# A graph network in four layers: the edge term of a pair added in one operation, sums of two pairs joined, weights stored behind the values

## The chip, the cores and the metric

The kernel runs on one core of a Trainium2 chip. The metric is the time on the device in microseconds; before the change it is 4184.97 us (median of 3 runs, 4182.91 to 4187.28).

## The reference

Four layers follow one another on 3125 nodes of 256 features and 53125 edges, sorted by destination. Each is `x = layernorm(x + layer(x))`. The change touches the fourth alone, two transformer convolutions with a ReLU between them, with 4 heads of 64 channels:

```python
def _transformer_conv(x, src, dst, edge_attr, Wq, bq, Wk, bk, Wv, bv, We, be, Ws, bs):
    q = (x @ Wq + bq).reshape(n, H, C)
    k = (x @ Wk + bk).reshape(n, H, C)
    v = (x @ Wv + bv).reshape(n, H, C)
    e = (edge_attr @ We + be).reshape(-1, H, C)
    k_j = k[src] + e
    q_i = q[dst]
    alpha = jnp.einsum('ehc,ehc->eh', q_i, k_j) / jnp.sqrt(C)
    ...
    msg = (v[src] + e) * alpha[..., None]
    out = jax.ops.segment_sum(msg, dst, num_segments=n)
    return out.reshape(n, H * C) + x @ Ws + bs
```

The dots stand for the softmax of `alpha` over the edges of one destination. The same edge term `e` is added to the key and to the value of an edge.

## The kernel before, in words

The program is a list of phases. The last five are `finish2` (end of the third layer, with the first projection), `attend(1)`, `between` (end of the first convolution, second projection), `attend(2)` and `last_rows`. A projection (`Projection`) makes queries, keys, values and skip terms; keys and values go to the table `kv_tab` in HBM, one row of 516 floats for a node: 256 of the key, then four heads of 64 value channels and one zero each (`KVW`, L42).

`attend` works on 440 tiles of 128 edges, two tiles making a pair, 220 pairs. A pair goes through these stations:

- The edge term, `aT` times `we`, is a product on TensorE into one of two PSUM banks (`edge_terms`, L1950).
- The gather of the 128 rows `kv_tab[src]` of a tile is an indirect DMA that GpSimd issues, one for a tile. There are two kinds. For an odd pair (`plain(p)`) it is plain (L1775): the rows land in the slots of `kv`, and VectorE adds the edge term afterwards, once to the keys (L1801) and once to the values (L1803). For an even pair ScalarE first copies the edge term twice into the slots (`fill`, L1890 and L1891), and the DMA accumulates onto it (L1779); VectorE adds nothing.
- TensorE picks the queries of the destinations with a one-hot matrix (`queries`, L1962), VectorE multiplies keys and queries (`times_q`, L1813) and sums over channels (`sum_channels`, L1819) into the scores.
- After 16 tiles (8 pairs) a softmax batch runs in small parts spread over three steps (`RunningSoftmax`, L1257 to L1314). Its weights are written by ScalarE into the slots, one behind the 64 channels of each head (`weights`, L1908).
- VectorE weighs the first two heads for 8 tiles at once (`weigh_first_heads`, L1827), ScalarE the other two (L1931).
- TensorE adds up the weighed values and weights of a tile by destination in a window of 128x260 (L1980, three PSUM banks), and VectorE adds each window to `acc` (`add_window`, L1849), whose block is chosen by a register.
- Once in a batch `acc` is rescaled (`rescale`, L1840).

Each engine has its own list of instructions, in the order in which the Python loops write them. Step `p` treats pair `p` up to the scores, and pair `p - 11` from the weights on. On VectorE a step is: the edge additions if the pair is plain, the multiplication, a part of the softmax, the first window, the channel sum, the second window, another part of the softmax, and where they fall due `rescale` and `weigh_first_heads`. A window waits for the window before it (`added`). The order of the edge products on TensorE comes from `edge_order`: that of an even pair is issued in step p - 6, that of a plain pair in step p - 1. GpSimd may issue the gathers of a plain pair when the slots are free (40 slots), those of an accumulating pair when ScalarE has filled them (`filled`); ScalarE fills five steps ahead.

Waits that are written in the code ahead of an instruction become semaphore conditions on it or on a small instruction before it:

```python
dve.wait_ge(products, t + 1)
if t > 0:
    dve.wait_ge(added, t)
...
nc.vector.tensor_tensor(window, window, PS[4 + t % WIN3][:, 0:LHW], ALU.add).then_inc(added, 1)
```

## Time and profile before

| | |
|---|---|
| runs | 4184.97 us (4182.91 to 4187.28) |
| profiled execution, its own time | 4176.55 us |
| its span, first to last instruction | 4174.8 us |
| granted TensorE clock, mean | 0.837 |
| busy: PE, DVE, ACT, POOL | 2915.8, 2728.3, 1937.5, 2545.6 us |
| first attention pass, gathers from, channel sums to | 2493.7, 3224.5 us |
| second attention pass, gathers from, channel sums to | 3370.0, 4101.7 us |

All rows are of one execution. PE is TensorE, DVE VectorE, ACT ScalarE, POOL GpSimd, SP the queue of plain DMAs; PEld is the loading of weights on TensorE. Shares over the whole span mix the three earlier layers, which the change does not touch, with the two attention passes; these take 1462 us of 4175. Idle time stands before the instruction that it precedes, with the event that ended it. "Issue" is idle time that the profile ties to no event.

### The profile page before, as it was taken

The numbers are of one execution on the slowest core, as the hardware profiler recorded it, in microseconds if no ns is written. First come the engines' busy times: TensorE is split into PE (matmuls) and PEld (weight loads), VectorE is DVE, ScalarE is ACT, GpSimd is POOL, SyncE is SP. The second block draws the span as 40 slices with busy tenths as digits, with TensorE's granted clock in tenths as the row PEclk, the third lists the DMA queues.
The fourth block names the chain that finished last, engine by engine and source line by source line (L and its number), as shares of the span: only waits on it lengthen the run. The fifth ranks groups of instructions, "written<-read, shape, count | busy, mean of one in ns | idle before, by whom it ended". The sixth has DMA issues, their size and how long they took to land. (4 is left out here: it accounts for less than half of the span.)

```text
span 4174.8 us, 55865 instructions
## 1 busy us (share of the span) xinstructions
PE 2915.8 (70%) x12421; PEld 2026.2 (49%) x12421; DVE 2728.3 (65%) x6440; ACT 1937.5 (46%) x5841; POOL 2545.6 (61%) x2336
## 2 busy tenths in 40 slices
PE   5466566267666695376767587888888878888884
PEld 3344444144444463244444235666665346666662
DVE  3455554545444445355555648999999669999997
ACT  2344344211111134132323446788787347788785
POOL 4666665366666400666666048888886268888881
PEclk7767777578888897677676789999999989999997
DMA  4645444366666621444444249999998489999993
GB/s 148 134 132 136 126 138 114 121 183 195 197 196 190 179 82 60 112 114 114 114 114 111 42 150 221 222 222 218 222 225 172 138 209 219 221 224 219 222 221 102
DMA packets 364138, 676.12 MB, mean 162 GB/s; under 512 B 65282, under 2 KB 167666, under 8 KB 363827
## 3 DMA queue, kind: packets, MB, share of 16 engines
q0 software_dynamic: 162048, 406.78, 43.6%
q1 hardware_dynamic: 197666, 261.96, 19.3%
q10 hardware_dynamic: 4112, 3.83, 0.3%
q8 instruction: 123, 2.02, 0.2%
q14 instruction: 189, 1.54, 0.1%
HBM read 582.61 MB, written 89.74 MB: 161 GB/s over the span
## 5 line engine op out<-in xcount | busy, mean ns | idle before, releaser
L1779 POOL DMA_INDIRECT t_kv<-kv_tab,srcT x440 | 712.1, 1618 | 152.5 <-issue 131.0
L1980 PE MATMUL bank<-t_kv,t_oh 128*128 128x260 f32 x1760 | 521.1, 406 | 146.2 <-DVE acc L1849 74.7
L1340 POOL DMA_INDIRECT grow<-h_tab,srcT x440 | 417.5, 949 | 285.0 <-issue 100.8
L493 POOL DMA_INDIRECT grow<-h_tab,srcT x440 | 428.8, 975 | 251.7 <-issue 109.7
L808 POOL DMA_INDIRECT grow<-x_tab,srcT x440 | 417.0, 948 | 243.7 <-issue 105.9
L1775 POOL DMA_INDIRECT t_kv<-kv_tab,srcT x440 | 466.0, 1059 | 134.1 <-issue 125.5
L1931 ACT ACTIVATE t_kv<-t_kv 128x64 f32<-128x64 f32 x1760 | 461.6, 333 | 0.0
L1950 PE MATMUL bank<-we,t_aT 128*128 128x256 f32 x1760 | 441.7, 391 | 21.0 <-DMA t_aT<-attrT_tab 20.7
L856 DVE TENSOR_TENSOR acc<-acc,bank 128x272 f32 x440 | 192.6, 438 | 383.7 <-PE bank L943 156.6
L943 PE MATMUL bank<-grow,oh 128*128 128x272 f32 x880 | 313.3, 480 | 184.6 <-issue 96.7
L1980 PEld LDWEIGHTS bank<-t_kv,t_oh 128*128 128x128 f32 x1760 | 287.7, 193 | 260.2 <-issue 133.3
L655 PE MATMUL bank<-grow,oh 128*128 128x258 f32 x880 | 333.3, 549 | 74.7 <-DVE acc L568 46.6
L1962 PE MATMUL bank<-H,t_ohT 128*128 x2640 | 368.4, 276 | 18.8 <-DVE t_ks L1813 18.0
L1849 DVE TENSOR_TENSOR acc<-acc,bank 128x260 f32 x880 | 364.8, 415 | 19.1 <-PE bank L1980 13.3
L1950 PEld LDWEIGHTS bank<-we,t_aT 128*128 128x128 f32 x1760 | 336.7, 197 | 71.7 <-DMA t_aT<-attrT_tab 22.4
L568 DVE TENSOR_TENSOR acc<-acc,bank 128x258 f32 x440 | 186.5, 424 | 282.0 <-PE bank L655 113.9
L1456 PE MATMUL bank<-grow,oh 128*128 128x257 f32 x880 | 340.7, 528 | 29.7 <-DVE acc L1382 17.5
L1813 DVE TENSOR_TENSOR t_ks<-t_kv,bank 128x512 f32<-128x512 f32 x440 | 299.0, 680 | 78.2 <-DMA t_kv<-kv_tab,srcT 75.0
L891 ACT COPY H<-bank 128x512 f32<-128x512 f32 x110 | 64.4, 585 | 604.9 <-DMA atail<-in_edge_attr 338.3
L1382 DVE TENSOR_TENSOR acc<-acc,bank 128x257 f32 x440 | 185.2, 421 | 233.7 <-PE bank L1456 94.5
L655 PEld LDWEIGHTS bank<-grow,oh 128*128 128x128 f32 x880 | 239.3, 284 | 145.4 <-ACT grow L630 51.6
L1962 PEld LDWEIGHTS bank<-H,t_ohT 128*128 128x128 bf16 x2640 | 256.3, 99 | 105.1 <-issue 26.9
(385 smaller groups left out, 5312.1 us busy)
## 6 DMA issues: line engine op xcount, KB each, us to landing
t_aT<-attrT_tab SPq DMA_DIRECT2D x110, 512.0 KB
H<-in_edge_attr SPq DMA_DIRECT2D x440, 64.0 KB
attrT_tab<-H SPq DMA_DIRECT2D x55, 512.0 KB
t_ohT<-place_tab SPq DMA_DIRECT2D x110, 256.0 KB
H<-lo_tab SPq DMA_DIRECT2D x55, 256.0 KB
grow<-h_tab,srcT POOLq DMA_INDIRECT x880
place_tab<-H SPq DMA_DIRECT2D x55, 256.0 KB
wbig<-place_tab SPq DMA_DIRECT2D x55, 256.0 KB
```

The costliest lines, as they stand in the source:

```text
L493: nc.gpsimd.indirect_dma_start(out=grow[:, t % RA, :], out_offset=None, in_=h_tab, in_offset=bass.IndirectOffsetOnAxis(ap=srcT[:, t:t + 1] ...
L655: nc.tensor.matmul(PS[t % WIN][:, 0:F + 2], oh[:, g % 2, u, :], grow[:, t % RA, :], start=True, stop=True).then_inc(products, 1)
L808: nc.gpsimd.indirect_dma_start(out=grow[:, t % RA, 0:F], out_offset=None, in_=x_tab, in_offset=bass.IndirectOffsetOnAxis(ap=srcT[:, t:t + ...
L1340: nc.gpsimd.indirect_dma_start(out=grow[:, t % R2, :], out_offset=None, in_=h2_tab, in_offset=bass.IndirectOffsetOnAxis(ap=srcT[:, t:t + 1 ...
L1456: nc.tensor.matmul(PS[2 + t % WIN2][:, 0:F + 1], oh[:, t // HB % 2, t % HB, :], grow[:, t % R2, 0:F + 1], start=True, stop=True).then_inc( ...
L1775: nc.gpsimd.indirect_dma_start(out=kv[:, u, :], out_offset=None, in_=kv_tab, in_offset=row).then_inc(g_ready[u], 16)
L1779: nc.gpsimd.indirect_dma_start(out=kv[:, u, :], out_offset=None, in_=kv_tab, in_offset=row, compute_op=ALU.add).then_inc(g_ready[u], 16)
L1849: nc.vector.tensor_tensor(window, window, PS[4 + t % WIN3][:, 0:LHW], ALU.add).then_inc(added, 1)
L1931: last = nc.scalar.activation(part, part, ACT.Copy, scale=u_rows[:, t % UB, h, C3:C3 + 1])
L1950: mm = nc.tensor.matmul(PS[j % 2][:, v * F:(v + 1) * F], aT[:, g % 3, u * P:(u + 1) * P], we[:, :], start=True, stop=True)
L1962: mm = nc.tensor.matmul(PS[2 + p % 2][:, v * F:(v + 1) * F], ohT[:, g % 3, u * P:(u + 1) * P], Q3[:, ds(blocks[u], 1), n, :].rearrange("p ...
L1980: nc.tensor.matmul(PS[4 + t % WIN3][:, 0:LHW], oh[:, t % OHS, :], kv[:, t % UB, F:KVW], start=True, stop=True).then_inc(products, 1)
```

## The change

It does five things in the fourth layer.

- The layout of a row of `kv_tab` and of `acc` is 256 key channels, 256 value channels in a row, then the 4 weights (before: each weight behind its head).
- The edge term is added to keys and values by one operation of 128x1024 on VectorE, reading the term twice; and ScalarE's two fills become one copy. One semaphore `edge_added` stands for `k_added` and `v_added`.
- The products with the queries of two pairs lie in one tile, and odd steps sum the channels of both pairs in one operation of 128x1024. Even steps sum nothing.
- `rescale` has one operation for the channels and one for the 4 totals.
- Pairs 8, 24, 40, ... 216, that is 14 of 220 in a pass, become plain.

```diff
-            return p % 2 == 1
+            return p % 2 == 1 or p % 16 == 8
...
-                ks = held(scope, f"{tag}_ks", [P, 2, 2, F])
+                u_rows = kv[:, :, F:2 * F].rearrange("p s (h c) -> p s h c", h=H3)
+                ks = held(scope, f"{tag}_ks", [P, 4, F])
...
-                            nc.vector.tensor_tensor(kv[:, s:s + 2, 0:F], kv[:, s:s + 2, 0:F], e, ALU.add).then_inc(k_added, 1)
-                            part = u_rows[:, s:s + 2, :, 0:C3]
-                            nc.vector.tensor_tensor(part, part, e.rearrange("p v (h c) -> p v h c", h=H3), ALU.add).then_inc(v_added, 1)
-                            dve.wait_ge(k_added, plains(p) + 1)
+                            part = kv[:, s:s + 2, 0:2 * F].rearrange("p v (a f) -> p v a f", a=2)
+                            nc.vector.tensor_tensor(part, part, e.unsqueeze(2).broadcast_to([P, 2, 2, F]), ALU.add).then_inc(edge_added, 1)
+                            dve.wait_ge(edge_added, plains(p) + 1)
...
-                                dve.wait_ge(sums_done, p - 1)
+                                dve.wait_ge(sums_done, p // 2)
...
-                        def sum_channels(p):
-                            b, i = 2 * p // NB, 2 * p % NB
-                            dve.wait_ge(q_used, p + 1)
-                            nc.vector.tensor_reduce(sm.al[:, b % 2, :, i:i + 2].rearrange("p h v -> p v h"), ks[:, p % 2, :, :].rearrange("p v (h c) -> p v h c", h=H3),
+                        def sum_channels(j):
+                            b, i = 4 * j // NB, 4 * j % NB
+                            dve.wait_ge(q_used, 2 * j + 2)
+                            nc.vector.tensor_reduce(sm.al[:, b % 2, :, i:i + 4].rearrange("p h v -> p v h"), ks[:, :, :].rearrange("p v (h c) -> p v h c", h=H3),
                                                     AX, ALU.add).then_inc(sums_done, 1)
...
-                            nc.vector.tensor_tensor(part, part, sm.fm[:, :].unsqueeze(2).broadcast_to([P, H3, C3 + 1]), ALU.mult).then_inc(sm.rescaled, 1)
+                            nc.vector.tensor_tensor(part, part, sm.fm[:, :].unsqueeze(2).broadcast_to([P, H3, C3]), ALU.mult)
+                            total = acc[:, ds(block_of_first, 1), F:LHW].rearrange("p a h -> p (a h)")
+                            nc.vector.tensor_tensor(total, total, sm.fm[:, :], ALU.mult).then_inc(sm.rescaled, 1)
...
-                            if p < PAIRS:
-                                sum_channels(p)
+                            if p < PAIRS and p % 2 == 1:
+                                sum_channels(p // 2)
...
-                            nc.scalar.copy(kv[:, u:u + 2, 0:F], e)
-                            nc.scalar.copy(u_rows[:, u:u + 2, :, 0:C3], e.rearrange("p v (h c) -> p v h c", h=H3)).then_inc(filled, 1)
+                            nc.scalar.copy(kv[:, u:u + 2, 0:2 * F].rearrange("p v (a f) -> p v a f", a=2), e.unsqueeze(2).broadcast_to([P, 2, 2, F])).then_inc(filled, 1)
```

The remaining lines of the diff follow the new layout (in `take`, `weights`, `weigh_first_heads`, the scaling on ScalarE, `sums_by_head` and the two memsets) or the new names and counts of semaphores.

How VectorE's list changes shows in two steps of the middle of a pass, a plain pair and the even pair after it. Before; the names behind "waits" are those under which the start of the program used the same semaphores: `up_row_spread` and `up_row_ready` are here `added` and `products`, `up_pads` is `q_used`, `up_packed` `k_added`, and the `ISA` rows set the address register of a window:

```order
L1801 TENSOR_TENSOR t_kv<-t_kv,bank 128x2x256 [waits g_ready35,g_ready34,up_ld_s]
L1803 TENSOR_TENSOR t_kv<-t_kv,bank 128x2x4x64
L1813 TENSOR_TENSOR t_ks<-t_kv,bank 128x512 [waits g_ready35,g_ready34,up_less_ready,up_consts,up_packed]
L1849 ISA [waits up_row_spread,up_row_ready]
L1849 TENSOR_TENSOR acc<-acc,bank 128x260
L1819 TENSOR_REDUCE t1s_al<-t_ks 128x2x4 [waits up_pads]
L1849 ISA [waits up_row_spread,up_row_ready]
L1849 TENSOR_TENSOR acc<-acc,bank 128x260
L1813 TENSOR_TENSOR t_ks<-t_kv,bank 128x512 [waits g_ready37,up_less_ready,g_ready36,up_consts]
L1849 ISA [waits up_row_spread,up_row_ready]
L1849 TENSOR_TENSOR acc<-acc,bank 128x260
L1819 TENSOR_REDUCE t1s_al<-t_ks 128x2x4 [waits up_pads]
```

Of the change, two such steps (L1811 is now the multiplication, L1817 the sum, `up_packed` is `edge_added`):

```order
L1801 TENSOR_TENSOR t_kv<-t_kv,bank 128x2x512 [waits g_ready11,g_ready10,up_ld_s]
L1811 TENSOR_TENSOR t_ks<-t_kv,bank 128x512 [waits g_ready11,g_ready10,up_less_ready,up_consts,up_packed]
L1849 ISA [waits up_row_spread,up_row_ready]
L1849 TENSOR_TENSOR acc<-acc,bank 128x260
L1817 TENSOR_REDUCE t1s_al<-t_ks 128x4x4 [waits up_pads]
L1849 ISA [waits up_row_spread,up_row_ready]
L1849 TENSOR_TENSOR acc<-acc,bank 128x260
L1811 TENSOR_TENSOR t_ks<-t_kv,bank 128x512 [waits g_ready13,up_less_ready,g_ready12,up_consts]
L1849 ISA [waits up_row_spread,up_row_ready]
L1849 TENSOR_TENSOR acc<-acc,bank 128x260
L1849 ISA [waits up_row_spread,up_row_ready]
L1849 TENSOR_TENSOR acc<-acc,bank 128x260
```

The multiplication now follows directly the addition whose result it waits for, and in the even step nothing stands between the two windows.

On GpSimd the gathers of pairs 7 to 9 in a pass change from plain, accumulating, plain. Of the change (L1774 is the plain gather, L1778 the accumulating one; `up_padded` is `filled`):

```order
L1778 DMA t_kv<-kv_tab,srcT 128x516 [waits up_padded]
L1778 DMA t_kv<-kv_tab,srcT 128x516
L1774 DMA t_kv<-kv_tab,srcT 128x516 x6
L1778 DMA t_kv<-kv_tab,srcT 128x516 [waits up_padded]
L1778 DMA t_kv<-kv_tab,srcT 128x516
```

Six plain gathers stand in a row where there were two, two accumulating ones and two.

## Rows read from the trace of the kernel before

**Rows 1.** Stretches: us; PE, PEld, DVE, ACT, POOL busy (instructions); clock; DMA share; GB/s.

```profile
2800.00:2900.00 100.00, 86.38 (x466) 64.89 (x464) 95.96 (x210) 81.28 (x257) 81.41 (x62) 0.98 0.97 223
...
3800.00:3900.00 100.00, 85.88 (x463) 64.70 (x464) 96.32 (x214) 79.11 (x252) 81.59 (x61) 0.98 0.95 216
```

**Rows 2.** Grouped lines by shape, 2700 to 3200 us: count, busy us, mean ns, idle, releasers.

```profile
L1779 POOL DMA_INDIRECT t_kv<-kv_tab,srcT x153 | 248.4, 1624 | 46.6 <-issue 45.4 <-ACT t_kv L1891 1.2
...
L1775 POOL DMA_INDIRECT t_kv<-kv_tab,srcT x152 | 161.0, 1059 | 46.3 <-issue 42.4 <-PE bank L1980 4.0
```

**Rows 3.** Timeline of POOL: start us, us, instruction, idle before it.

```profile
2848.24 1.57 POOL L1779 DMA_INDIRECT t_kv<-kv_tab,srcT  x1 [0.30 <-issue]
2850.11 1.55 POOL L1779 DMA_INDIRECT t_kv<-kv_tab,srcT  x1 [0.30 <-issue]
2851.97 1.00 POOL L1775 DMA_INDIRECT t_kv<-kv_tab,srcT  x1 [0.30 <-issue]
2853.27 0.97 POOL L1775 DMA_INDIRECT t_kv<-kv_tab,srcT  x1 [0.31 <-issue]
2854.55 1.57 POOL L1779 DMA_INDIRECT t_kv<-kv_tab,srcT  x1 [0.30 <-issue]
```

**Rows 4.** Timeline of POOL, second pass.

```profile
3967.26 2.37 POOL L1779 DMA_INDIRECT t_kv<-kv_tab,srcT  x1 [0.30 <-issue]
```

**Rows 5.** Timeline of DVE, one block of the second pass, no row of which has idle time.

```profile
3957.59 0.68 DVE L1813 TENSOR_TENSOR t_ks<-t_kv,bank 128x512 f32<-128x512 f32 x1
...
3960.80 0.67 DVE L1801 TENSOR_TENSOR t_kv<-t_kv,bank 128x512 f32<-128x512 f32 x1
...
3961.99 0.67 DVE L1813 TENSOR_TENSOR t_ks<-t_kv,bank 128x512 f32<-128x512 f32 x1
...
3964.61 0.28 DVE L1305 TENSOR_REDUCE t2s_d<-bank 128x64 f32<-128x128 f32 x1
3964.93 0.23 DVE L1308 TENSOR_TENSOR t2s_d<-t2s_al,t2s_d 128x64 f32<-128x64 f32 x1
3965.10 0.69 DVE L1813 TENSOR_TENSOR t_ks<-t_kv,bank 128x512 f32<-128x512 f32 x1
3965.71 0.42 DVE L1849 TENSOR_TENSOR acc<-acc,bank 128x260 f32 x1
3966.04 0.68 DVE L1819 TENSOR_REDUCE t2s_al<-t_ks 128x8 f32<-128x512 f32 x1
3966.64 0.42 DVE L1849 TENSOR_TENSOR acc<-acc,bank 128x260 f32 x1
3966.97 1.22 DVE L1827 TENSOR_TENSOR t_kv<-t_kv 128x1024 f32<-128x1024 f32 x1
3968.11 0.68 DVE L1801 TENSOR_TENSOR t_kv<-t_kv,bank 128x512 f32<-128x512 f32 x1
...
3979.78 0.68 DVE L1801 TENSOR_TENSOR t_kv<-t_kv,bank 128x512 f32<-128x512 f32 x1
...
3982.84 0.68 DVE L1813 TENSOR_TENSOR t_ks<-t_kv,bank 128x512 f32<-128x512 f32 x1
```

**Rows 6.** Source lines L1819, L1813: ns min/median/max, starts; idle before L1813 and its releaser.

```profile
L1819 DVE TENSOR_REDUCE t1s_al<-t_ks x220: 661/679/689, 2501.9 to 3224.5; 128x8 f32<-128x512 f32 x110
...
  DMA t_kv<-kv_tab,srcT: 75.0, 31
```

**Rows 7.** Timeline of DVE, two multiplications with the queries that follow a wait.

```profile
2553.41 0.69 DVE L1813 TENSOR_TENSOR t_ks<-t_kv,bank 128x512 f32<-128x512 f32 x1 [0.99 <-DMA t_kv<-kv_tab,srcT]
...
4011.12 0.69 DVE L1813 TENSOR_TENSOR t_ks<-t_kv,bank 128x512 f32<-128x512 f32 x1 [2.33 <-DMA t_kv<-kv_tab,srcT]
```

**Rows 8.** Timeline of DVE, last windows of the first pass.

```profile
3238.35 0.43 DVE L1849 TENSOR_TENSOR acc<-acc,bank 128x260 f32 x1 [0.21 <-PE bank L1980]
3238.99 0.43 DVE L1849 TENSOR_TENSOR acc<-acc,bank 128x260 f32 x1 [0.21 <-DVE acc L1849]
```

**Rows 9.** Timeline of PE, the block of rows 5.

```profile
3976.60 1.89 PE L1950 MATMUL bank<-we,t_aT 128*128 128x256 f32 x8
```

More of the change, by code:

```diff
@@ L1553, in begin @@
                 step(nc.vector.tensor_tensor(b_all[:, 2 * F:3 * F], b_all[:, 2 * F:3 * F], self.b_e[:, :], ALU.add))
-                step(nc.vector.memset(self.kv[:, :, :, F:KVW].rearrange("p q n (h c) -> p (q n) h c", h=H3)[:, :, :, C3:C3 + 1], 0.0))
+                step(nc.vector.memset(self.kv[:, :, :, 2 * F:KVW], 0.0))
             def take(self, dve, t):
@@ L1752, in attend @@
             tag = f"t{layer}"
-            names = "oht_in0 oht_in1 oht_in2 at_in0 at_in1 at_in2 oh_ready e_ready filled q_ready q_used sums_done msg_ready act_ready products added zeroed k_added v_added dve act".split()
+            names = "oht_in0 oht_in1 oht_in2 at_in0 at_in1 at_in2 oh_ready e_ready filled q_ready q_used sums_done msg_ready act_ready products added zeroed edge_added dve act".split()
             (oht_in0, oht_in1, oht_in2, at_in0, at_in1, at_in2, oh_ready, e_ready, filled, q_ready, q_used, sums_done, msg_ready, act_ready,
-             products, added, zeroed, k_added, v_added, dv, ac) = [sem(f"{tag}_{n}") for n in names]
+             products, added, zeroed, edge_added, dv, ac) = [sem(f"{tag}_{n}") for n in names]
             oht_in, at_in = (oht_in0, oht_in1, oht_in2), (at_in0, at_in1, at_in2)
@@ L1823, in weigh_first_heads @@
                             dve.wait_ge(sm.w_ready, g // 2 + 1)
-                            dve.wait_ge(v_added, plains(4 * g + 4))
+                            dve.wait_ge(edge_added, plains(4 * g + 4))
                             u = g * HB % UB
-                            part, weights = u_rows[:, u:u + HB, 0:DVE_HEADS, 0:C3], u_rows[:, u:u + HB, 0:DVE_HEADS, C3:C3 + 1]
+                            part, weights = u_rows[:, u:u + HB, 0:DVE_HEADS, :], kv[:, u:u + HB, 2 * F:2 * F + DVE_HEADS].unsqueeze(3)
                             nc.vector.tensor_tensor(part, part, weights.broadcast_to([P, HB, DVE_HEADS, C3]), ALU.mult).then_inc(msg_ready, 1)
@@ L1907, in weights @@
                                 u = (b * NB + i) % UB
[L1908 removed]
+                                last = nc.scalar.activation(kv[:, u:u + HB, 2 * F:KVW],
                                                             sm.d[:, :].rearrange("p (h i) -> p i h", h=H3)[:, i:i + HB, :], ACT.Exp)
@@ L1926, in _ @@
                                     act.wait_ge(sm.w_ready, q // 8 + 1)
-                                    act.wait_ge(v_added, plains(min(PAIRS, q + 8)))
+                                    act.wait_ge(edge_added, plains(min(PAIRS, q + 8)))
                                 for t in range(2 * q, 2 * q + 2):
                                     for h in range(DVE_HEADS, H3):
-                                        part = u_rows[:, t % UB, h, 0:C3]
-                                        last = nc.scalar.activation(part, part, ACT.Copy, scale=u_rows[:, t % UB, h, C3:C3 + 1])
+                                        part = u_rows[:, t % UB, h, :]
+                                        last = nc.scalar.activation(part, part, ACT.Copy, scale=kv[:, t % UB, 2 * F + h:2 * F + h + 1])
                                     last.then_inc(act_ready, 1)
@@ L1944, in edge_terms @@
                                 if plain(last):
-                                    pe.wait_ge(v_added, plains(last) + 1)
+                                    pe.wait_ge(edge_added, plains(last) + 1)
                                 else:
@@ L1985, in _ @@
                             if batch:
-                                sm.pe(pe, batch[0], 2 * batch[1], sums_done, min(PAIRS, 8 * batch[0] + 8))
+                                sm.pe(pe, batch[0], 2 * batch[1], sums_done, min(PAIRS // 2, 4 * batch[0] + 4))
                             if p + AHEAD + 1 < PAIRS and not plain(p + AHEAD + 1):
@@ L2003, in sums_by_head @@
         def sums_by_head(step, i, q, den, r):
-            sums = group(acc, i)[:, :, 0:LHW].rearrange("p n (h c) -> p n h c", h=H3)
-            step(nc.vector.tensor_scalar(den[:, q, 0, :, :], sums[:, :, :, C3], 1.0e-16, None, ALU.add))
+            sums = group(acc, i)[:, :, 0:F].rearrange("p n (h c) -> p n h c", h=H3)
+            step(nc.vector.tensor_scalar(den[:, q, 0, :, :], group(acc, i)[:, :, F:LHW], 1.0e-16, None, ALU.add))
             step(nc.vector.reciprocal(den[:, q, 1, :, :], den[:, q, 0, :, :]))
             for n in range(GRP):
-                last = nc.vector.tensor_tensor(r[:, n, :].rearrange("p (h c) -> p h c", h=H3), sums[:, n, :, 0:C3],
+                last = nc.vector.tensor_tensor(r[:, n, :].rearrange("p (h c) -> p h c", h=H3), sums[:, n, :, :],
                                                den[:, q, 1, n, :].unsqueeze(2).broadcast_to([P, H3, C3]), ALU.mult)
```

11 lines of the change are left out of this document (4 added, 7 removed).

## The prediction

> **What bounds the kernel now.** The change touches only the fourth layer, which runs twice, so I first cut the span into stretches [rows 1]. In the two attention passes no engine is free: of 100 us VectorE (DVE) is busy 96 us and more, TensorE (PE) 85, ScalarE (ACT) 80, GpSimd (POOL) 81, the granted TensorE clock is 0.98 to 1.00, the DMA engines are busy 95 to 97%. Busy shares alone would name DVE. The grouped lines say otherwise [rows 2]: in 500 us POOL issues 153 accumulating gathers (248.4 us) and 152 plain ones (161.0 us), and stands idle 46.6 + 46.3 us before them, nearly all of it put down to "issue". 248.4 + 161.0 + 46.6 + 46.3 = 502 us, so POOL has no time left. Its timeline shows what the idle time is [rows 3]: before every gather 0.30 us, and no more. POOL works through its list without a pause, 6.31 us for two pairs (2848.24 to 2854.55): one pair accumulating (2 x (1.57 + 0.30)), one plain (2 x (1.0 + 0.30)). Now and then a gather is stretched: one of 2.37 us in place of 1.57 [rows 4] lies beside DVE's 128x1024 product of values and weights, L1827 [rows 5]. That the DMA engines are so busy does not show as a limit of its own: POOL is never held back, and the change moves no byte more.
>
> DVE follows closely. Between 3957.59 and 3982.84 us its timeline runs one whole block of 8 pairs with one softmax batch and not one idle gap: 25.25 us [rows 5]. That is DVE's own pace. The average is slower: the channel sums of the first pass start at 2501.9 and at 3224.5 us with 219 pairs between them [rows 6], 26.40 us a block. The block after the full one contains a wait of 2.33 us for a gather [rows 7]; all such waits of the products with the queries are 75.0 us [rows 6]. So the passes go at POOL's pace (25.25 us a block plus about 1 us of stretched gathers), and DVE has a reserve of 26.40 - 25.25 = 1.15 us a block. **The question is whether the change adds more than that to DVE.**
>
> **The change, part by part, for a block of 8 pairs.** Every DVE price below is start to start, because neighbours that wait for nothing overlap: an operation of 0.68 us lets the next one start after 0.60, one of 0.42 after 0.33 [rows 5].
>
> *Edge term in one operation.* Two 128x512 additions and the start of the product behind them take 3960.80 to 3961.99, 1.19 us [rows 5]. Now it is one of 128x1024. The nearest row is L1827, as many elements: 1.22 us long [rows 5]. The product with the queries reads what it wrote and waits for it, where before it waited only for the first of the two. The softmax pair L1305, L1308 shows such a wait: 0.28 us long, successor 0.32 us after its start, so a gap of 0.04 [rows 5]. Hence 1.22 + 0.04 = 1.26, +0.07 for each of 4 plain pairs: +0.28. Bounds: without any wait the next operation starts 1.14 after L1827 (-0.05 each); at worst the gap is 0.21, as between windows below (+0.24 each).
>
> *One more plain pair in sixteen.* Pairs 8, 24, ... 216, 14 in each pass, now need the addition on DVE: 1.26 us in every second block, +0.63. On POOL each saves 2 x (1.57 - 1.0) = 1.15 us, 0.57 a block or 16 us a pass. ACT loses 14 fills a pass. PE issues the same matmuls, only later (the edge product of pair 8 in step 7, not 2).
>
> *Channel sums of two pairs at once.* An odd step has a sum of 128x1024 in place of 128x512: the next operation starts 1.14 us after it, not 0.60: +0.54, four times, +2.16. An even step loses its sum, and with it what lay between its two window additions. Before: first window, sum, second window, 3965.71 to 3966.64, 0.93 us [rows 5]. Now the second window follows the first directly and waits for it (`added`), then sets registers for its address. This succession stands in the trace at the end of the pass, where no sums are left: 3238.35, 3238.99, 0.64 us apart although one takes 0.43, the gap of 0.21 put down to the window before [rows 8]. In the middle of the pass the window takes 0.42, so 0.63. The even step saves 0.30 and not 0.60: -1.20 a block. All told the joined sum costs DVE +0.96 a block: the wait that the sum had hidden comes into the open, since 1024 channels saved no element of work.
>
> *Factor for channels and weight totals apart.* One 128x260 operation becomes 128x256 and 128x4. They wait for nothing of each other. The nearest row for the small one is L1308, 64 elements, whose successor starts 0.17 after it [rows 5]; with 60 fewer elements I take 0.10, between nothing and the 0.32 of L1305, which is waited for.
>
> *Free or beside the path.* ACT makes one copy of 128x1024 where it made two; it is busy 80 us of 100 [rows 1] and comes out no slower. The layout itself (values contiguous, weights behind them) changes no element count; the zeroing at the start and the row phases between are as long as before. The multiplication of an even step now waits for a long sum, but a window addition lies between, and it starts 1.14 + 0.33 us after the sum, which takes 1.22.
>
> *Sum.* +0.28 + 0.63 + 2.16 - 1.20 + 0.10 = +1.97. DVE's own pace goes from 25.25 to 27.22 us; POOL needs 26.40 - 0.57 = 25.83. **DVE becomes the bound**, POOL gets ahead until the fills hold it, and the waits for gathers vanish. The first two blocks keep POOL's pace (windows begin only at step 12): pair 16 is multiplied at 2553.41 [rows 7]. From there to 3224.5 are 203 pairs (with one sum behind it), 25.4 blocks in 670.2 us, 26.4 each. At 27.22 they take 691.4, +21.2 us. I add nothing for new PE waits (below) and take off nothing; two passes give +42 us. The profiled execution took 4176.55 us (span 4174.8), 0.2% under the median of the runs, 4184.97. From the first that makes 4219, and from the median, with which a measurement will be compared, **4227 us, 1.0% slower**. About 0.2% is what a measurement of this kernel can tell from no change.
>
> **A rule weighed against a row.** The trace has two windows 0.64 us apart where a wait lies between them [rows 8] and one with none ahead of the sum at 0.33 (3965.71 to 3966.04) [rows 5]. The Trainium skill, VectorE: DVE Perf Modes, section "The DRAIN you can't avoid", reports eight copies equally long with a semaphore after each or only after the last: "the semaphore costs nothing extra here"; its rules for kernel authors advise to minimize the count of operations, not of semaphores. By that rule the change, which takes six or seven of DVE's some fifty-five operations from a block, would be a gain. It is rival B.
>
> **The rivals.**
> B, *waits cost DVE nothing* (ends faster). The second window follows at 0.33, the product follows the edge term at 1.14. Then the block changes by -0.20 (edge, four times -0.05) + 0.57 (new plain) + 2.16 - 2.40 (even steps without 0.60) + 0.10 = +0.23: 25.48, below POOL's 25.83. POOL stays the bound and its 14 x 1.15 us a pass are the gain: 2 x 16 = 32 us, 4153. It decides below 25.83, that is below +0.58. For it: only end-of-pass rows show the window latency. Against it: the same instruction, the same wait. The trace of this kernel so far speaks against the page's rule; chance 0.12.
> C, *DVE at its new pace waits for PE besides* (slower still). Work on DVE is now uneven, an even step some 0.3 us shorter and an odd one 0.6 longer. PE ends eight edge matmuls at 3976.60 + 1.89 = 3978.49 [rows 9], and DVE takes the edge term at 3979.78 [rows 5]: a reserve of 1.3 us. Where a softmax batch begins, the score transposes wait for the sum, which now ends 0.54 later. If this leaks 0.6 us a block, it adds 15 us a pass: 4257. Chance 0.10.
> D, *the window latency is hidden in the middle of the pass, but the other terms hold*: 27.22 - 1.20 = 26.02, just over POOL's 25.83; with small waits as now, about 26.3, equal to now: 4180. Chance 0.08.
>
> **How the numbers follow.** Forecast A 0.70, B 0.12, C 0.10, D 0.08. A's own range: the edge wait between its bounds (-0.4 to +0.8 a block), the small factor up to +0.26, some PE waits: 4212 to 4255. Taking in C and the upper part of D: 4190 to 4262. Left out are B, half of D and the far edge, under 0.2. Slower by over 0.2%: A, C, 0.80. Within: 0.08, D mostly. Faster: 0.12, B.
>
> **What would show it.** Right: POOL's idle time before gathers is no longer 0.30 each but waits for ACT's fills, and the stretch with no DVE idle is a block of about 27.2 us everywhere; waits of the products for gathers fall from 75 us to a few; merged addition 1.22 us, its successor 1.26 after it; in even steps windows 0.63 apart; the sum 1.22 us; each pass about 21 us longer. Wrong: windows 0.33 apart in even steps, POOL still at 0.30 throughout and a shorter pass (B); DVE idle growing before windows or edge terms with PE as releaser (C); a merged addition far from 1.22 us.

## The result, and the profile after

The changed kernel takes 4269.87 us (4263.41 to 4270.67) beside 4185.32 us of the kernel before (4182.91 to 4187.28, 4 runs): a ratio of 1.0194, 95% interval 1.0177 to 1.0211, 84.5 us slower. A fourth, slow run took 5965.8 us and is in neither the range nor the ratio (without it the median is 4269.07). The forecast was 4227 in a range of 4190 to 4262: the direction is right, the size is half of what came, and the time lies just outside the range. The profiled execution took 4263.41 us, span 4261.6, granted clock 0.838.

The stretches [rows 1], after:

```profile
2800.00:2900.00 100.00, 81.71 (x434) 60.83 (x433) 93.92 (x172) 74.47 (x228) 73.56 (x58) 0.98 0.89 211
3800.00:3900.00 100.00, 82.20 (x443) 60.77 (x444) 94.88 (x179) 75.69 (x233) 76.81 (x61) 1.00 0.90 211
```

POOL was busy 81 us of 100 and is busy 74 and 77; ACT, too, has more time left. The grouped lines by shape, 2700 to 3200 us [rows 2]:

```profile
L1778 POOL DMA_INDIRECT t_kv<-kv_tab,srcT x128 | 202.9, 1585 | 76.6 <-ACT t_kv L1890 43.3 <-issue 33.3
L1774 POOL DMA_INDIRECT t_kv<-kv_tab,srcT x162 | 172.1, 1062 | 49.4 <-issue 45.7 <-PE bank L1979 3.7
...
L1849 DVE TENSOR_TENSOR acc<-acc,bank 128x260 f32 x292 | 122.3, 419 | 16.7 <-DVE acc L1849 12.3 <-issue 3.6 <-PE bank L1979 0.2
...
L1801 DVE TENSOR_TENSOR t_kv<-t_kv,bank 128x1024 f32<-128x1024 f32 x83 | 100.6, 1212 | 2.2 <-DMA atail<-in_edge_attr 2.1
...
L1817 DVE TENSOR_REDUCE t1s_al<-t_ks 128x16 f32<-128x1024 f32 x73 | 88.6, 1214 | 0.0
...
L1890 ACT COPY t_kv<-bank 128x1024 f32<-128x1024 f32 x64 | 64.4, 1007 | 74.9 <-PE bank L1949 71.9 <-issue 2.9
```

POOL now stands idle 76.6 us before 128 accumulating gathers, 43.3 of it for ACT's fills, and ACT waits 71.9 us for edge products: POOL is ahead and is held back. Over the whole run the multiplication waits 32.0 us for gathers where it waited 75.0, and 27.7 of that are the two waits at the start of a pass (14.3 and 13.4). DVE's prices stand in its timeline [rows 5], a plain step, an even one and the next plain one:

```profile
2639.33 1.21 DVE L1801 TENSOR_TENSOR t_kv<-t_kv,bank 128x1024 f32<-128x1024 f32 x1
2640.58 0.69 DVE L1811 TENSOR_TENSOR t_ks<-t_kv,bank 128x512 f32<-128x512 f32 x1
2641.18 0.42 DVE L1849 TENSOR_TENSOR acc<-acc,bank 128x260 f32 x1
2641.52 1.22 DVE L1817 TENSOR_REDUCE t1s_al<-t_ks 128x16 f32<-128x1024 f32 x1
2642.64 0.41 DVE L1849 TENSOR_TENSOR acc<-acc,bank 128x260 f32 x1
2642.98 0.68 DVE L1811 TENSOR_TENSOR t_ks<-t_kv,bank 128x512 f32<-128x512 f32 x1
2643.57 0.42 DVE L1849 TENSOR_TENSOR acc<-acc,bank 128x260 f32 x1
2644.20 0.43 DVE L1849 TENSOR_TENSOR acc<-acc,bank 128x260 f32 x1 [0.21 <-DVE acc L1849]
2644.55 1.22 DVE L1825 TENSOR_TENSOR t_kv<-t_kv 128x1024 f32<-128x1024 f32 x1
2645.68 1.22 DVE L1801 TENSOR_TENSOR t_kv<-t_kv,bank 128x1024 f32<-128x1024 f32 x1
2646.93 0.69 DVE L1811 TENSOR_TENSOR t_ks<-t_kv,bank 128x512 f32<-128x512 f32 x1
```

Edge term to multiplication 1.25 us (forecast 1.26), sum to window 1.12 (1.14), window to window in the even step 0.63 (0.63). All of it came as written. The split factor costs 0.06 to 0.07 us a batch (0.10): from its first operation to the multiplication behind it 0.41 us, where the single operation had 0.34 to 0.35. What was not written is in two other rows of DVE:

```profile
2587.56 0.69 DVE L1811 TENSOR_TENSOR t_ks<-t_kv,bank 128x512 f32<-128x512 f32 x1 [3.55 <-DMA afix<-tail_tab]
2588.41 0.42 DVE L1849 TENSOR_TENSOR acc<-acc,bank 128x260 f32 x1 [0.16 <-DMA place_tab<-H]
```

This multiplication of pair 22 (the names of the DMAs are those under which an early phase used the same semaphores) waits 3.55 us. The last updates that the trace holds for its two gathers stand at 2578.9 and 2579.7 (5 of 16 each; the trace of this chip lacks the others). TensorE's records have the products with its queries soon after:

```profile
2578.95 0.82 PE L1961 MATMUL bank<-H,t_ohT 128*128 x6
2579.61 1.04 PE L1979 MATMUL bank<-t_kv,t_oh 128*128 128x260 f32 x4
2580.48 0.82 PE L1961 MATMUL bank<-H,t_ohT 128*128 x6
2581.14 0.60 PE L1979 MATMUL bank<-t_kv,t_oh 128*128 128x260 f32 x2
```

The query products by the record end at 2581.3, but the semaphore that announces them is updated at 2587.54, and DVE starts at 2587.56: it did wait for TensorE, whose signal came 6.2 us behind the recorded end. The granted clock was 1.00 while DVE waited and fell only afterwards, to 1.2 GHz for 3.4 us from 2591.2 on:

```profile
2588.00:2592.00 4.00, 2.50 (x11) 1.65 (x12) 2.92 (x5) 2.85 (x8) 2.98 (x3) 0.90 0.88 190
2592.00:2600.00 8.00, 6.78 (x31) 4.34 (x29) 7.65 (x17) 5.83 (x19) 5.60 (x6) 0.84 0.95 236
```

The block of pairs 16 to 24 takes 33.5 us, in both passes; some others take 29.45 in place of 27.8, with a wait of 0.9 to 1.2 us before an edge addition (2695.05, 2751.03, 2807.14):

```profile
2695.05 1.22 DVE L1801 TENSOR_TENSOR t_kv<-t_kv,bank 128x1024 f32<-128x1024 f32 x1 [1.19 <-DMA atail<-in_edge_attr]
```

Here, too, the signal of the edge product is late: recorded end 2692.61, signal 2695.03. In blocks without such a wait the multiplications are 26.53 or 27.82 us apart, mean 27.18. So a pass, from the multiplication of pair 16 to that of pair 216, takes 692.5 and 697.9 us (658.4 and 659.3 before), where 25 x 27.18 = 679.5 were to be had. The two passes are 72.7 us longer together, and the first gather comes 9.2 us later; that is 82 of the 86.8 us between the two spans.

### The profile page after: what moved, and what is told of

Read it like the earlier page. It is cut to its first block and busy times, and to the rows that moved or that the text cites. A ratio compares the mean times of both kernels' runs of the same rounds, so it can differ in the third digit from the quotient of the medians.

```text
span 4261.6 us, 55319 instructions
## 1 busy us (share of the span) xinstructions
PE 2937.8 (69%) x12421; PEld 2028.2 (48%) x12421; DVE 2772.9 (65%) x6084; ACT 1896.0 (44%) x5593; POOL 2493.2 (59%) x2336
## 5 line engine op out<-in xcount | busy, mean ns | idle before, releaser
L1778 POOL DMA_INDIRECT t_kv<-kv_tab,srcT x384 | 609.7, 1588 | 235.7 <-ACT t_kv L1890 133.4
L1774 POOL DMA_INDIRECT t_kv<-kv_tab,srcT x496 | 518.9, 1046 | 151.2 <-issue 140.5
L1456 PE MATMUL bank<-grow,oh 128*128 128x257 f32 x880 | 333.6, 519 | 27.8 <-DVE acc L1382 16.9
L1811 DVE TENSOR_TENSOR t_ks<-t_kv,bank 128x512 f32<-128x512 f32 x440 | 301.6, 686 | 55.1 <-DMA t_kv<-kv_tab,srcT 32.0
L1890 ACT COPY t_kv<-bank 128x1024 f32<-128x1024 f32 x192 | 193.4, 1007 | 290.9 <-PE bank L1949 259.3
L1801 DVE TENSOR_TENSOR t_kv<-t_kv,bank 128x1024 f32<-128x1024 f32 x248 | 300.8, 1213 | 25.4 <-DMA t_kv<-kv_tab,srcT 12.0
```

Of the source, the lines that this page charges most:

```text
L1456: nc.tensor.matmul(PS[2 + t % WIN2][:, 0:F + 1], oh[:, t // HB % 2, t % HB, :], grow[:, t % R2, 0:F + 1], start=True, stop=True).then_inc( ...
L1774: nc.gpsimd.indirect_dma_start(out=kv[:, u, :], out_offset=None, in_=kv_tab, in_offset=row).then_inc(g_ready[u], 16)
L1778: nc.gpsimd.indirect_dma_start(out=kv[:, u, :], out_offset=None, in_=kv_tab, in_offset=row, compute_op=ALU.add).then_inc(g_ready[u], 16)
```

## The experiments

The first four kernels separate the prices; the others follow what did not fit. All ratios are to the kernel before on the same chip. The chips turned out not to be alike, so each heading says which: **S** is a chip on which before takes 4168 us (e1 to e4; the result above is from one of 4185), **Q** one of 3871 to 3874 (four chips). Each chip has runs of one time only, so what is called the chip here may be something else that was different then. The letter has nothing to do with the "theory S" of some expectations, which is the burst of gathers. "A pass" is the time from pair 16 to pair 216, first and second pass of the profiled execution.

### e1 (S): no extra plain pair

```diff
-            return p % 2 == 1 or p % 16 == 8
+            return p % 2 == 1
```

> The changed kernel without its extra plain pairs: 8, 24, 40 and so on accumulate again, all else stays. Theory 1 (VectorE's own pace is the sum of its prices, and the stalls beyond it, a block of 33.5 us about pair 22 and six blocks of 29.45 us, come from three plain pairs in a row, whose edge products TensorE issues late): every block is the kind without the extra addition, 26.53 us in the changed kernel's trace, the stalls are gone, and a pass from the multiplication of pair 16 to that of pair 216 takes 25 x 26.53 = 663 us, against 658.4 before and 692.5 changed. Time: the changed kernel's 4270 less 2 x 30, about 4210. Rival (the stalls come from the joined sum, whose scores reach TensorE later, or from the uneven steps): the block about pair 22 still takes 33 us, a pass 675 to 680 us, the time 4235 to 4245. The first gather of pass 1 tells of the 9 us lost ahead of it: 2503 if the changed layout or code carries them, 2494 if the extra pairs do.

4205.99 us, ratio 1.0096 (1.007 to 1.0123); passes 674.7 and 671.6 us, first gather at 2488.8. No wait at pair 22. Blocks are 26.53, or 27.68 where the operation L1285 of the softmax waits 0.55 us more for TensorE: the odd step's long sum, I take it, lets TensorE start late. The forecast had that as part of rival C. Against 25 x 26.53 = 663.3 the passes are 8 to 11 us longer.

### e2 (S): a sum in every step

```diff
-                            if p < PAIRS and p % 2 == 1:
-                                sum_channels(p // 2)
+                            if p < PAIRS:
+                                sum_channels(p)
```

(and `sum_channels` of one pair, with its counts.)

> The changed kernel with a channel sum in every step, one pair each, as before; layout, merged edge term and extra plain pairs stay. Theory 1 (the joined sum costs VectorE 0.96 us a block, since it takes the filler from between the two windows; the stalls come from the extra plain pairs): blocks of 25.6 and 26.9 us, mean 26.2, in even steps the windows 0.93 apart again with the sum between them, the block about pair 22 still long; a pass is 24 us shorter than the changed kernel's 692.5, 668 us; time about 4220. Rival (the joined sum also causes the stalls): the stalls go too, a pass takes 25 x 26.2 = 656 us, time about 4195. Rival (waits cost nothing, joining saved instructions): windows no closer to free than now, the time at or above 4270.

4208.39 us, ratio 1.0108 (1.0076 to 1.0139); blocks 25.6 and 27.25, passes 670.6 and 686.2. An even-pair block is 0.93 us shorter than the change's 26.53, near the forecast 0.96, but the passes are only 22 and 12 us shorter where 24 were expected: waits before the edge addition at pair 5 of each sixteen (1.1 us in the mean) stay, and in the second pass nine of 25 blocks take 28.7 us or more. The clean price is that of g1.

### e3 (S): the kernel before, with the extra plain pairs alone

```diff
-            return p % 2 == 1
+            return p % 2 == 1 or p % 16 == 8
```

> The kernel before with one edit, the extra plain pairs 8, 24, 40 and so on. GpSimd needs 25.83 us a block in place of 26.40, VectorE 25.25 and 26.44 in turn, mean 25.85. Theory 1a (prices alone): a pass 25 x 25.9 = 648 us against 658.4 before, the time 4165, faster by 20. Theory 1b (three plain pairs in a row make TensorE's products late whatever VectorE does): the block about pair 22 shows a wait of 3 to 4 us and others of 1.2 us, 9 to 17 us a pass, which takes the gain back: 4180 to 4195. Rival (the stalls need the slower VectorE of the changed kernel): no stall, as 1a. The first gather of pass 1 is at 2494.

4209.93 us, ratio 1.0106 (1.0084 to 1.0128), passes 676.7 and 675.3. 1b, and worse: blocks with the extra pair take 28.6 us in the mean, not 26.44. DVE's timeline at pair 133:

```profile
2943.27 0.69 DVE L1813 TENSOR_TENSOR t_ks<-t_kv,bank 128x512 f32<-128x512 f32 x1
2944.79 0.42 DVE L1849 TENSOR_TENSOR acc<-acc,bank 128x260 f32 x1 [0.83 <-PE bank L1980]
```

TensorE's timeline ahead of it:

```profile
2939.26 1.89 PE L1950 MATMUL bank<-we,t_aT 128*128 128x256 f32 x8
2940.99 0.82 PE L1962 MATMUL bank<-H,t_ohT 128*128 x6
2941.64 1.04 PE L1980 MATMUL bank<-t_kv,t_oh 128*128 128x260 f32 x4
```

The window needs a product that TensorE's record ends at 2942.7 at the latest; DVE gets it at 2944.79. Six plain gathers in a row were issued from 2934.1 to 2942.3. Its stretches, with the columns of [rows 1], show 362 GB/s where 220 are usual, and a granted clock of 1.00 throughout:

```profile
2936.00:2940.00 4.00, 2.82 (x14) 2.02 (x15) 3.86 (x9) 2.96 (x11) 3.21 (x3) 1.00 1.05 362
2938.00:2946.00 8.00, 5.67 (x31) 4.58 (x32) 7.02 (x16) 6.17 (x21) 6.47 (x6) 1.00 0.82 246
```

### e4 (S): the first window ahead of the multiplication

```diff
+                            if 1 <= q:
+                                add_window(first, blocks[first % HB])
                             if p < PAIRS:
...
                                 times_q(p)
...
-                                add_window(first, blocks[first % HB])
+                                add_window(first + 1, blocks[(first + 1) % HB])
                             if p < PAIRS and p % 2 == 1:
                                 sum_channels(p // 2)
-                            if 1 <= q:
-                                add_window(first + 1, blocks[(first + 1) % HB])
```

The second window moves too, ahead of the channel sum, which the expectation does not say.

> The changed kernel with the first window addition moved ahead of the multiplication with the queries, so that this lies between the two windows and the first window lies between the edge term and the multiplication that waits for it. Theory 1 (the joined sum lost 0.30 us in each even step to the latency between two windows, and the merged edge term some 0.1 us in each plain step): windows no longer 0.63 apart with nothing between, a block 1.2 to 1.5 us shorter, 25.7 to 26.0 in place of 27.2, near GpSimd's 25.83; a pass some 30 us shorter if the stalls stay, the time about 4210, and down to 4180 if they go. Rival (the latency between windows is not what costs, VectorE's element work is): within 5 us of 4270.

4234.42 us, ratio 1.0168 (1.014 to 1.0196), passes 690.9 and 690.3. About 4210 was expected. The interval overlaps that of the change (1.0177 to 1.0211), so no gain is shown, and the waits are in it; see g2.

### e5 to e7 (Q): GpSimd's order

```diff
+                        gather_order = list(range(ET // 2))
+                        for n in range(8, ET // 2 - 2, 16):
+                            gather_order[n:n + 3] = [n + 2, n, n + 1]
-                        for t in range(ET):
+                        for t in (2 * n + v for n in gather_order for v in range(2)):
```

(e5 on e3's kernel, e6 on the changed one; e7 on e1's with `[n + 1, n + 3, n, n + 2]` for four pairs.)

> The kernel before with the extra plain pairs, as in e3, but GpSimd gathers pair 10 (accumulating) ahead of pairs 8 and 9, and so for 26, 42 and on: four plain gathers in a row in place of six. TensorE's, VectorE's and ScalarE's lists are those of e3. Theory S (six plain gathers in a row are a burst of writes of 375 GB/s, in which TensorE's matmuls, already let go, end 1 to 3 us late): the idle time of VectorE at pairs 5 and 6 of each sixteen, 1.14 + 0.53 us in e3, falls under 0.4, a pass from pair 16 to 216 takes 650 to 660 us in place of 676, the time is 25 to 40 us under e3's, that is 0.997 to 1.004 of before. Theory T (the changed order of the edge products on TensorE is what comes late): the same waits as e3, ratio 1.010.

> The changed kernel with the same exchange in GpSimd's list, pair 10 ahead of 8 and 9 in every sixteen. Theory S (burst): a pass without the long block about pair 22 and without the blocks of 29.45 us, 25 blocks of 27.2, 680 us in place of 692 to 698; ratio to before 1.012 to 1.014 in place of 1.019, since VectorE's own pace of 27.2 us a block is left. Theory T: unchanged, 1.019.

> The kernel of e1 (changed kernel without extra plain pairs) with GpSimd's list alone reordered: in every sixteen it gathers pairs 7, 9, 11, 8, 10 in place of 7, 8, 9, 10, 11, so that six plain gathers stand in a row. No other engine's list changes and no work is added; gathers lead their use by 16 us, so that none comes too late. Theory S (burst): VectorE waits 1 to 1.5 us for TensorE once in sixteen pairs where e1 had nothing, a pass is 10 to 20 us longer than e1's 672 to 675, the time 20 to 35 us over e1's. Theory T (edge order): same as e1 within 5 us.

e5: 3931.43 us, 1.0144 (1.0124 to 1.0165), passes 684.5 and 689.4. A poor test: there are no waits at pairs 5 and 6 (f1 will show none on Q without the exchange either), but pair 8 now comes late, since its gather stands behind one that waits for a fill. DVE's waits, 2300 to 2900 us (waited for: us in total, times, longest):

```profile
DVE t_kv L1804 <- DMA t_kv<-kv_tab,srcT: 26.1, 11, 3.1
```

e6: 3954.49 us, 1.0209 (1.0187 to 1.023), passes 688.4 and 694.4; no long block at pair 22, the same new wait. e7: 3914.96 us, 1.0105 (1.0084 to 1.0127), passes 670.4 and 672.1, no wait at all beside the burst. On Q, then, the burst alone brings no wait. That says nothing of S: f1 shows that on Q the waits of e3 are absent in e3's own kernel.

### e8 (Q): the kernel before

> The kernel before, unchanged, profiled on the same chip as its neighbours: how long its passes and the phases ahead of them are there. All theories: ratio 1.000; passes from pair 16 to 216 of 658 to 660 us as in the first profile. If the 9 us ahead of the first pass in the changed kernel's profile were its own, this one's first gather lies some 9 us before that of the kernels with the changed layout; if they were the chip's and the run's spread, it lies among the 2483 to 2489 us of e1 to e4.

3873.84 us, ratio 0.9994. The passes take 656.5 and 660.3 us as on the first chip, but the first gather stands at 2192.7 us, 301 us earlier. This chip gains all of its 300 us ahead of the passes. Two of the three source lines of GpSimd's gathers in the earlier layers (ns min/median/max, starts), of before on the first chip:

```profile
L493 POOL DMA_INDIRECT grow<-h_tab,srcT x440: 941/949/8143, 60.7 to 709.7; - x147
...
L1340 POOL DMA_INDIRECT grow<-h_tab,srcT x440: 941/949/1122, 1666.6 to 2304.2; - x147
```

and on this one:

```profile
L493 POOL DMA_INDIRECT grow<-h_tab,srcT x440: 942/946/8786, 61.3 to 623.0; - x147
...
L1340 POOL DMA_INDIRECT grow<-h_tab,srcT x440: 942/946/1174, 1456.1 to 2005.7; - x147
```

The same 440 gathers of 0.95 us take 649 us on the one and 562 on the other; in the second layer 640 and 549, in the third 638 and 550. That is 266 of the 301 us; the other 35 lie between these phases. They gather plainly throughout. The granted clock in them is lower on the first chip, too: 0.70, 0.81 and 0.70 against 0.73, 0.92 and 0.76; whether that is a cause or comes of TensorE's idle time is not shown. DVE's window additions in the first of them, timeline on the first chip:

```profile
399.83 0.42 DVE L568 TENSOR_TENSOR acc<-acc,bank 128x258 f32 x1 [0.66 <-issue]
401.60 0.42 DVE L568 TENSOR_TENSOR acc<-acc,bank 128x258 f32 x1 [1.35 <-issue]
403.74 0.42 DVE L568 TENSOR_TENSOR acc<-acc,bank 128x258 f32 x1 [1.72 <-PE bank L655]
```

TensorE's timeline there:

```profile
398.29 4.66 PE L655 MATMUL bank<-grow,oh 128*128 128x258 f32 x14
```

DVE's on this chip:

```profile
400.08 0.42 DVE L568 TENSOR_TENSOR acc<-acc,bank 128x258 f32 x1 [0.21 <-PE bank L655]
400.71 0.42 DVE L568 TENSOR_TENSOR acc<-acc,bank 128x258 f32 x1 [0.21 <-PE bank L655]
401.35 0.42 DVE L568 TENSOR_TENSOR acc<-acc,bank 128x258 f32 x1 [0.21 <-DVE acc L568]
401.99 0.42 DVE L568 TENSOR_TENSOR acc<-acc,bank 128x258 f32 x1 [0.21 <-DVE acc L568]
```

On the first chip DVE gets a product each 1.8 to 2.1 us while TensorE's record shows 14 matmuls, seven products, within 4.66 us without a pause; on this one they follow each other at DVE's own 0.64. So TensorE's products come late on that chip in the unchanged phases too, and its recorded ends don't show it.

The semaphore updates in the traces do, and they part the chips cleanly. In the three earlier layers the updates by which TensorE announces a window's product should be 0.43 us apart or more, as the recorded ends are. In the six traces from the slower chips (before, the change, e1 to e4) 285 to 347 of some 1030 recorded updates come less than 0.15 us behind the one before: they arrive in bunches, and so late. In the fourteen traces on Q not one of some 1320 does. In the first pass of e8, f1 and f3 TensorE's updates stand at most 16 ns behind the recorded ends, and VectorE's and ScalarE's updates at most 13 ns behind theirs on either kind of chip; it is TensorE's alone that are late. On the slower chips the update of an edge product is over 0.5 us late 15 times in the first pass of the change, 20 in e2, 15 in e3 and 17 in e4, and never in before and e1 (of 111 to 157 that each of these traces holds).

On the 9 us ahead of the first pass: over all profiles on Q the first gather starts at 2191.4 to 2202.6 us with the changed layout and at 2191.0 to 2199.8 without, on the chip of e1 to e4 at 2483.2 to 2488.8 and 2486.5. The spread covers any share of the change.

### e9 to e12 (Q): TensorE's work put back

```diff
-                            for v in range(2):
+                            for v in range(2) if p % 16 != 3 or p + 5 >= PAIRS else (0, 1, 0, 1):
                                 u = (2 * p + v) % HB
                                 mm = nc.tensor.matmul(PS[j % 2]...
```

(e9 on e3's kernel, e12 on the changed one; e10 is e3 with `gather_order[n:n + 2] = [n + 1, n]` for n = 22, 38, ...; e11 is both.)

> The kernel of e3 (before plus the extra plain pairs) with TensorE's lost work put back: in the step where the edge product of pair 8 of each sixteen stood, the edge product of the plain pair 3 is computed twice into the same bank, so that TensorE has as much to do there as before; the product of pair 8 itself stays in its later step. No other engine's list changes. Theory U (TensorE, left with less work in that stretch, comes late three steps on, at pairs 5 and 6): the 1.14 + 0.53 us of VectorE's idle time there fall under 0.4, a pass from pair 16 to 216 takes 650 to 658 us in place of 676, ratio to before 0.995 to 1.001 in place of 1.0106. Theory S' (the burst of six plain gathers together with the later product of pair 8): same waits as e3, ratio 1.010 or more, since TensorE has more to do.

> The kernel of e3 with GpSimd gathering the plain pair 7 ahead of the accumulating pair 6 in every sixteen from pair 22 on, so that two plain pairs, one accumulating, two plain ones follow each other: four plain gathers in a row and no gather put back by more than one pair. In e5 the wait at pair 5 was gone, but pair 8 came late by 2 to 4 us. Theory S' (burst): the waits at 5 and 6 vanish and none takes their place, 650 to 658 us a pass, ratio 0.995 to 1.001. Theory U (less work on TensorE): same waits as e3, ratio 1.010.

> Both edits, e9's doubled product and e10's exchanged gathers. If either cause is the whole, it equals the better of e9 and e10; if both are needed, it alone reaches 650 us a pass and a ratio of 0.995. If neither counts, 1.010.

> The changed kernel with e9's doubled product. Theory U: no block of 29.45 us and none of 33.5 about pair 22, 25 blocks of 27.2, 680 us a pass in place of 692 to 698, ratio 1.012 to 1.014. Theory S': as the changed kernel, 1.019.

e9: 3858.02 us, ratio 0.9965 (0.9952 to 0.9978), passes 651.5 and 649.3. e10: 3860.7 us, 0.998 (0.9969 to 0.9991), 650.0 and 649.2. e11: 3861.43 us, 0.9976 (0.9963 to 0.9988), 650.9 and 650.2. e12: 3927.09 us, 1.0145 (1.0121 to 1.017), 681.7 and 683.2. Each looked like a cure, two unlike cures equally good and both together no better. That is suspicious, and e8 had shown that these chips differ from S.

### f1 to f4 (Q): cure and patient on one chip

f1 is e3's kernel again, f2 e9's, f3 the changed kernel, f4 e12's.

> The kernel of e3 again (before plus the extra plain pairs), on the same chip as the next three. e3 and its cure e9 ran on different chips, and these differ: before took 4168 us on the one and 3871 on the other. Theory U (TensorE's missing work or the burst brings the waits): VectorE waits at pairs 5 and 6 of each sixteen here too, a pass takes 670 to 677 us, ratio to before 1.008 to 1.012. Rival K (the waits at pairs 5 and 6 belong to the slower chips, not to the kernel): on a chip where before takes 3870 to 3875 us no such wait, 648 to 652 us a pass and a ratio of 0.996, the same as e9; on one of 4170 to 4185 the waits of e3.

> The kernel of e9 (e3 with the doubled edge product of pair 3) again. Theory U: on any chip 649 to 652 us a pass, ratio 0.9965, some 1.3% under f1. Rival K: equal to f1 within 0.2%.

> The changed kernel itself again. Theory U: blocks of 29.45 us and the long one about pair 22, 692 to 698 us a pass, ratio 1.019 or more. Rival K: on a fast chip 680 to 684 us a pass as e12 had, ratio 1.0145.

> The kernel of e12 (changed kernel with the doubled product) again. Theory U: 680 to 684 us a pass on any chip, ratio 1.0145, 0.5% under f3. Rival K: equal to f3.

| | ratio, 95% interval | passes, us |
|---|---|---|
| f1, extra pairs | 0.9963 (0.9951 to 0.9975) | 649.6, 648.1 |
| f2, the same, doubled product | 0.9966 (0.9955 to 0.9977) | 650.6, 648.5 |
| f3, the changed kernel | 1.0148 (1.0128 to 1.0168) | 681.5, 684.1 |
| f4, the same, doubled product | 1.0155 (1.0134 to 1.0176) | 681.4, 683.7 |

On Q rival K holds: the doubled product cures nothing, the waits are not there to be cured. For its other half, the waits on a slower chip, only the earlier e3 stands; none of the four kernels was run on S again. The same six gathers in a row in f1, its stretch:

```profile
2625.00:2629.00 4.00, 2.70 (x13) 1.93 (x14) 3.86 (x9) 3.07 (x12) 3.32 (x3) 1.00 1.04 353
```

DVE's timeline at the same pair 133:

```profile
2632.32 0.68 DVE L1813 TENSOR_TENSOR t_ks<-t_kv,bank 128x512 f32<-128x512 f32 x1
2632.92 0.41 DVE L1849 TENSOR_TENSOR acc<-acc,bank 128x260 f32 x1
```

TensorE's, ahead of it:

```profile
2630.76 1.04 PE L1980 MATMUL bank<-t_kv,t_oh 128*128 128x260 f32 x4
```

353 GB/s, the products by the record done at 2631.8, and the window follows 0.60 after the multiplication. **The extra plain pairs alone make the kernel 0.4% faster on Q and 1.1% slower on S.**

### g1 and g2 (Q): the prices without the waits

g1 is e2, g2 is e4, both with e9's doubled product.

> The kernel of e2 (changed kernel, channel sums of one pair in every step) with e9's doubled product. On a fast chip (before some 3870 us): blocks of 25.6 and 26.9 us without waits, 25 x 26.25 = 656 us a pass, which is before's own length there (656.5 and 660.3), ratio 0.998 to 1.002; so the joined sum alone is worth 25 us a pass of the changed kernel's 682. On a slow chip (before some 4170 to 4185 us): if the doubled product cures the waits at pairs 4 to 6 of e2, the same 656 us; if it doesn't, 670 to 686 us as in e2 and a ratio of 1.011.

> The kernel of e4 (changed kernel, the first window ahead of the multiplication) with e9's doubled product. On a fast chip: no window directly behind another in an even step, 1.2 us off a block, 27.2 becomes 26.0, near GpSimd's 25.83: 650 to 660 us a pass, ratio 0.996 to 1.003, if nothing else comes to wait; e4's blocks on the slow chip held 0.3 to 0.6 us more, at the start of the softmax batches, so 660 us is the likelier end. On a slow chip: with the cure 655 to 665 us, without it 690 as e4.

g1: 3872.39 us, ratio 1.0002 (0.999 to 1.0013), passes 656.1 and 657.3: the joined sum is worth 26 us a pass. So all of the change but the joined sum equals before, its gain and its costs about cancelling: on Q the joined sum is the whole loss. Against f2 (extra pairs and doubled product, without the merged edge term, the layout and the split factor) g1's passes are 7 us longer, 0.29 a block, where the forecast had 0.28 + 0.10. g2: 3931.18 us, 1.0156 (1.0134 to 1.0178), passes 681.6 and 683.3: nothing gained over f4, a miss. The window no longer follows a window, but:

```profile
2581.39 1.20 DVE L1801 TENSOR_TENSOR t_kv<-t_kv,bank 128x1024 f32<-128x1024 f32 x1
2582.73 0.42 DVE L1849 TENSOR_TENSOR acc<-acc,bank 128x260 f32 x1
2583.08 0.68 DVE L1811 TENSOR_TENSOR t_ks<-t_kv,bank 128x512 f32<-128x512 f32 x1
```

a window behind the merged addition starts 1.34 us after it (1.34 at the least in all 234 such places), where the multiplication started 1.25 after it and 1.14 was expected without a wait; why is not shown, and a window has waits of its own; and L1285 at the start of a batch waits up to 1.2 us for TensorE. Blocks take 26.1 to 26.5 and 27.6 us where f4 has 26.54 and 27.8, and some of 29 take that back.

## Why the prediction was half right

The direction and the prices on VectorE were right; 4269.87 us lies outside the range, and the loss is twice the forecast one.

*Bound of the kernel: right.* POOL's pace set the passes before, DVE's sets them after; POOL now waits for fills, and the waits for gathers are nearly all at the starts of the passes.

*DVE's own pace, 25.25 to 27.22 us: right.* Measured 27.18; edge step 1.25 for 1.26, windows 0.63, split factor 0.06 to 0.07 for 0.10, mean of f3's 25 blocks 681.5 / 25 = 27.26. On Q the profiled pair f4 and e8 lies 50.9 us apart in span, 48.3 of it in the two passes; the sum had +42, because it took 26.4 us a block for before where Q's passes show 26.26 and 26.41, and left out the softmax waits of e1. The ratio there, 1.0148, is 57 us by the medians.

*The joined sum costs +0.96 a block: right,* g1 against f4, 25.3 and 26.4 us a pass, 1.03 a block.

*The extra plain pair: right in its price* (+1.19 to 1.29 in every second block), and on Q its gain shows once nothing else is changed: 25.85 forecast for DVE, 25.95 measured in f1 (648.9 / 25), 14 us under before in all.

*Rival B (a wait costs nothing; the Trainium skill, VectorE: DVE Perf Modes, "The DRAIN you can't avoid"): wrong here.* The Trainium skill reports there of eight copies that "the semaphore costs nothing extra here". In this kernel's timeline two windows with a wait between them are 0.63 us apart, and with an operation behind the window that does not wait for it 0.33 to 0.35; and g1, with more operations than the change, is faster.

**The step that failed is "I add nothing for new PE waits".** On the chip of record they are 13 us in the first pass and 18 in the second (692.5 and 697.9 against 679.5). Of these 2 and 5 are there on Q as well (f3: 681.5 and 684.1); the other 11 and 14 are of the slower chip alone. Rival C had a leak of 0.6 us a block and 4257 us, the nearest number, and 31 us in 50 blocks are 0.6 a block; that is luck, for it came by another road: it looked for DVE's unevenness against TensorE's 1.3 us of reserve [rows 9]. In e3 the waits come although VectorE's list has none of the joined operations. What came is a lag of TensorE's signals behind its own recorded ends, of 2 to 6 us, in the kernels with six plain gathers in a row, and on the slower chips alone. The rest of the 84.5 us is 9 ahead of the passes, no more than the spread between profiles, and the terms above.

*What stays open.* That bursts of plain gathers bring the lag on S is an argument: it comes where they stand (e3, e2, the changed kernel; not in e1), and the phases with plain gathers only are those in which S is slow. The extra plain pairs also move the edge product of pair 8 to a later place in TensorE's list, and on S nothing separates the two: no kernel with reordered gathers, and none with the doubled product, ran there. What differs in the chips is not shown. The granted clock does not explain the waits in the passes (1.00 in e3 beside the wait at 2944.79, 1.00 before pair 22 in the change); in the earlier layers it is lower on S.

## What to carry to other kernels

Joining operations on a tight engine pays only if they leave no latency bare: count what stood between two dependent operations before taking it away. Here the joined sum saved 110 operations a pass and cost 26 us. When a change's loss has two parts, one of them may belong to the chip; profile the kernel before on every chip, and measure a cure and its patient on one chip. A profile's matmul ends are modelled: where a waiting engine starts well after them, with all its other inputs there, believe the waiting engine, and look at when the semaphore was updated.

## What was not expected of the hardware

- The same program takes 8% longer on one chip than on another (4185 and 3874 us). 266 of 301 us lie in phases of plain gathers (649 and 562 us for 440 gathers of 0.95 us each), none in the passes with accumulating ones between (658.4 and 656.5 us). The gathers are equally long; what comes late is TensorE's signals, 311 of 1026 of them within 0.15 us of the one before, where the faster chip has none of 1320.
- The same edit, fourteen pairs in a pass, changes sign between them: 1.0106 and 0.9963.
- An addition of 128x1024 from PSUM lets a dependent multiplication start after 1.25 us and a window addition, which works on another tile, only after 1.34.
